# Layer 1's attention: dividing the head outputs by their sums behind the value product, instead of the probabilities before it

## The reference

```
q = (layernorm(x) @ wq + bq)  -> (16, 16 heads, 256, 8)
k = (ctx @ wk + bk)           -> (16, 16 heads, 64, 8)
v = (ctx @ wv + bv)           -> (16, 16 heads, 64, 8)
scores = q k^T / sqrt(8)
attn = softmax(scores, axis=-1)          # over 64 keys
out = attn v                             # (16, 256, 16 heads x 8 = 128)
x = x + tanh(g_xattn[1]) * (out @ wo + bo)
```

## Time and profile before

| | |
|---|---|
| median of 3 runs | 1190.56 us (1184.3 to 1193.06) |
| profiled execution | 1190.58 us, span 1188.8 us |
| mean granted clock of TensorE | 0.93 of full |
| busy: PE, DVE, ACT, POOL | 1069.7, 896.4, 578.6, 699.2 us |
| of POOL: L783, all four layers, 128 times | 215.6 us |
| layer 1: first and last residual update (L1307) | 212.08 and 400.96 us from the span's start |

### The profile page before, as it was taken

The page is one execution under the profiler, slowest core; times in us unless marked ns, Lnnn a source line. Parts: engine busy times, 40 slices in busy tenths (PEclk is TensorE's granted clock), DMA queues, the critical chain, the costliest instruction groups (busy, mean ns, idle before and its releaser), DMA issues. The chain is left out here.

```text
span 1188.8 us, 22954 instructions
## 1 busy us (share of the span) xinstructions
PE 1069.7 (90%) x6913; PEld 764.1 (64%) x6914; DVE 896.4 (75%) x2320; ACT 578.6 (49%) x1268; POOL 699.2 (59%) x979
## 2 busy tenths in 40 slices
PE   7999886888888899999999997999999999999643
PEld 5666574555555678957777766779966666666413
DVE  3999866788898668677788887667667777777395
ACT  2555443555555334455455553235445555554564
POOL 2555553666578764378766778844237677775203
PEclk7999996799889799999999999999999999999755
DMA  7997020000000016500000000025300000000002
GB/s 199 379 398 288 1 82 1 1 2 1 2 19 23 30 57 161 161 16 22 21 22 18 26 19 28 30 68 140 94 8 21 21 19 19 19 8 1 1 0 71
DMA packets 71551, 74.10 MB, mean 62 GB/s; under 512 B 9866, under 2 KB 57492, under 8 KB 71316
## 3 DMA queue, kind: packets, MB, share of 16 engines
q1 hardware_dynamic: 65300, 60.13, 15.8%
q0 software_dynamic: 6144, 12.64, 3.6%
HBM read 26.97 MB, written 45.78 MB: 61 GB/s over the span
## 5 line engine op out<-in xcount | busy, mean ns | idle before, releaser
L783 POOL TENSOR_TENSOR arena<-arena,zinv 128x1024 f32<-128x1024 f32 (+1 forms) x128 | 215.6, 1685 | 106.8 <-DVE zinv L1383 106.0
L1298 DVE TENSOR_REDUCE nmax<-S 128x16 f32<-128x1024 f32 (+1 forms) x128 | 138.8, 1084 | 101.9 <-PE S L2020 98.8
L2020 PEld LDWEIGHTS OX<-arena,pT 128*128 128x128 f32 x1280 | 151.6, 193 | 45.5 <-issue 44.9
L2020 PE MATMUL OX<-arena,pT 128*128 128x128 f32 x1280 | 166.3, 282 | 5.8 <-ACT pT L1072 5.7
L2020 PE MATMUL S<-arena,xT 128*128 128x512 f32 (+1 forms) x320 | 161.1, 602 | 1.1 <-ACT arena L1042 0.8
L1072 ACT ACTIVATE pT<-PT 128x512 f32<-128x512 f32 x224 | 124.6, 596 | 64.8 <-PE PT L2235 64.2
L2235 PE MATMUL PT<-ident,arena 128*128 128x128 f32 x896 | 132.5, 292 | 19.4 <-POOL arena L783 18.7
L2235 PEld LDWEIGHTS PT<-ident,arena 128*128 128x128 f32 x896 | 105.3, 148 | 54.6 <-POOL arena L783 37.9
L1358 DVE TENSOR_REDUCE zsum<-arena 128x16 f32<-128x1024 f32 (+1 forms) x128 | 137.7, 1076 | 0.0
L1349 DVE TENSOR_TENSOR arena<-S,nmax 128x1024 f32<-128x1024 f32 (+1 forms) x128 | 136.0, 1063 | 0.0
L1001 ACT ACTIVATE arena<-arena 128x1024 f32<-128x1024 f32 (+1 forms) x128 | 120.7, 943 | 6.9 <-DVE arena L1349 6.9
(11 more groups left out here) (374 smaller groups left out, 2324.6 us busy)
## 6 DMA issues: line engine op xcount, KB each, us to landing
x_sorted<-q_in SPq DMA_DIRECT2D x37, 387.0 KB, 4.8
y_sorted<-q_in SPq DMA_DIRECT2D x37, 384.0 KB, 4.7
arena<-x_sorted SPq DMA_DIRECT2D x62, 129.0 KB, 2.3
y_sorted<-arena SPq DMA_DIRECT2D x62, 128.0 KB, 2.1
x<-in_x SPq DMA_DIRECT2D x4, 512.0 KB, 7.8
out<-x SPq DMA_DIRECT2D x8, 256.0 KB, 2.3
moe_flat<-y_sorted,pos POOLq DMA_INDIRECT x96, 2.6
moe_flat<-in_L_gate_up_T SPq DMA_DIRECT2D x1, 1280.0 KB, 6.8
```

Source lines behind the costliest of these rows:

```text
L783: pool.tensor_tensor(pr, pr, z, ALU.mult).then_inc(s.probs_done, 1)
L1298: dve.tensor_reduce(nmax[:, p, 0:H], S[p][:, 0:W].rearrange("p (h k) -> p h k", h=H), AX.X, ALU.max, negate=True).then_inc(s.max_done, 1)
L2020: return pe.matmul(out, lhsT, rhs, start=start, stop=stop)
```

## The change

In layer 1 alone:

- POOL no longer multiplies the probabilities (32 instructions of 128 x 1024). `turn` waits for ACT's exponentials (`exp_done`) instead of for POOL.
- DVE no longer sums over the keys (L1358) and takes no reciprocal of 16 sums (L1383).
- PE multiplies the transposed probabilities a second time, behind the value product, with a constant of zeros and ones (`v1_ones`, 128 x 64): 8 matmuls of 32 columns into `GV[:, 128:256]`. Each of the 128 rows there is the sum of the head to which that row of `GV[:, 0:128]` belongs, so each head's sum is written 8 times. `attn_done` comes behind this second product.
- DVE, first thing in the next step, takes the reciprocal of 128 x 128 from `GV` into `attnT` and multiplies `GV[:, 0:128]` by it; `output1` waits for that (`sums_applied`). ACT's copy to `attnT` goes.
- POOL writes the constant between layer 0 and layer 1: one memset of 128 x 64 and four of 64 x 8.

```diff
@@ DVE, step t of layer 1 @@
+                    if a.small and is_tile(t - 1):
+                        heads = attnT[:, (r + 3) % 2, :]
+                        dve.wait_ge(s.attn_done, t)
+                        done(dve, s.out_done, a.tile0 + t - 3)
+                        dve.reciprocal(heads, GV[:, P:2 * P]).then_inc(s.head_sums_inverted, 1)
+                        dve.wait_ge(s.head_sums_inverted, t)
+                        dve.tensor_tensor(heads, GV[:, 0:P], heads, ALU.mult).then_inc(s.sums_applied, 1)
                     if a.small:
                         score_max()
...
-                    if is_tile(n):
+                    if is_tile(n) and not a.small:
                         T, p, j = a.tile0 + n, (r + 1) % 2, (r + 1) % 4
                         dve.wait_ge(s.exp_done, T + 1)
                         dve.tensor_reduce(zsum[:, p, 0:H], probs[:, j, 0:W].rearrange("p (h k) -> p h k", h=H), AX.X,
...
@@ POOL @@
-                    if is_tile(n):
-                        done(pool, s.zinv_done, a.tile0 + n)
+                    if is_tile(n) and not a.small:
+                        done(pool, s.sums_applied, a.tile0 + n)
                         pr = probs[:, (r + 1) % 4, 0:a.H * KEYS].rearrange("p (h k) -> p h k", h=a.H)
...
             pool.memset(v1, 0.0).then_inc(s.v1_zeroed, 1)
+            pool.memset(v1_ones[:, :], 0.0).then_inc(s.v1_zeroed, 1)
+            pool.wait_ge(s.v1_zeroed, 2)
+            for e in range(2):
+                for half in range(2):
+                    pool.memset(v1_ones[64 * e:64 * e + 64, 48 * half + 8 * e:48 * half + 8 * e + 8], 1.0).then_inc(s.v1_zeroed, 1)
+                    pool.wait_ge(s.v1_zeroed, 3 + 2 * e + half)
@@ ACT @@
-                    if a.small and is_tile(t):
-                        done(act, s.attn_done, t)
-                        done(act, s.out_done, a.tile0 + t - 2)
-                        act.activation(attnT[:, r % 2, :], GV[:, 0:P], ACT.Copy).then_inc(s.attn_evac, 1)
@@ PE: output1, heads1, turn @@
-                        pe.wait_ge(s.attn_evac, t)
+                        pe.wait_ge(s.sums_applied, a.tile0 + t)
...
+                        for c in range(8):
+                            rows = slice(32 * (c % 4), 32 * (c % 4) + 32)
+                            at = 32 * (c // 4)
+                            ins = mm(GV[rows, P:2 * P], v1_ones[:, at:at + 32], pT[:, r % 2, P * c:P * c + P],
                                      start=c < 4, stop=c >= 4)
                         ins.then_inc(s.attn_done, 1)
...
-                        pe.wait_ge(s.probs_done, a.tile0 + t + 1)
+                        if a.small:
+                            pe.wait_ge(s.exp_done, a.tile0 + t + 1)
+                        else:
+                            pe.wait_ge(s.probs_done, a.soft0 + t + 1)
```

More of the change, by code:

```diff
@@ L60, in __init__ @@
         self.small = dh < KEYS
+        self.soft0 = TILES * (l - (l > 1))
         self.gfill0 = BATCHES * sum(b.halves for b in before if not b.small)
@@ L172, in __init__ @@
         self.attn_done = sem("attn_done")
-        self.attn_evac = sem("attn_evac")
+        self.head_sums_inverted = sem("head_sums_inverted")
         self.kT_done = sem("kT_done")
@@ L194, in __init__ @@
         self.sum_done = sem("sum_done")
-        self.zinv_done = sem("zinv_done")
+        self.sums_applied = sem("sums_applied")
         self.probs_done = sem("probs_done")
@@ L430, in flamingo_program @@
         nmax = sb("nmax", [P, 2, 16])
+        v1_ones = sb("v1_ones", [P, 64])
         zsum = sb("zsum", [P, 2, 16])
@@ L1051, in filled @@
                                 act.wait_ge(s.sides_made, 4)
-                                act.wait_ge(s.v1_zeroed, 1)
+                                act.wait_ge(s.v1_zeroed, 6)
                             for e in range(2):
@@ L1379, in step @@
                         routing(a.l, t, 3)
[L1380 to L1383, removed]
+                    if is_tile(t + 1) and not a.small:
+                        dve.wait_ge(s.sum_done, a.soft0 + t + 2)
+                        done(dve, s.probs_done, a.soft0 + t - 1)
+                        dve.reciprocal(zinv[:, p, 0:H], zsum[:, p, 0:H]).then_inc(s.sums_applied, 1)
                     if between:
@@ L2185, in heads1 @@
                             ins = mm(GV[rows, 0:P], v1[:, (r // 2) % 2, at:at + 32], pT[:, r % 2, P * c:P * c + P],
+                                     start=c < 4, stop=c >= 4)
+                        for c in range(8):
+                            rows = slice(32 * (c % 4), 32 * (c % 4) + 32)
+                            at = 32 * (c // 4)
+                            ins = mm(GV[rows, P:2 * P], v1_ones[:, at:at + 32], pT[:, r % 2, P * c:P * c + P],
                                      start=c < 4, stop=c >= 4)
```

## The result

| | before | changed |
|---|---|---|
| median | 1189.47 us (1184.3 to 1193.06, 4 runs) | 1176.13 us (1173.19 to 1177.82, 4 runs) |
| profiled execution, span | 1190.58, 1188.8 us | 1177.82, 1176.1 us |
| mean granted clock | 0.93 | 0.951 |
| busy: PE, DVE, ACT, POOL | 1069.7, 896.4, 578.6, 699.2 us | 1058.7, 902.1, 571.4, 638.8 us |

The ratio of changed to before is 0.9895, with a 95% interval of 0.9866 to 0.9924: faster, by 1.0%. The forecast was 1178.6.

The account below looks back on a forecast made before the run. Bound: DVE's own work plus the ring through POOL. Tile 2 to 28: 43.2 + 99.0 + 2.6 = 144.8 against 158.9, -14.1; end +2.1; together -12.0 from 1190.58 gives 1178.6 us, range 1170 to 1190.

Parts of the forecast that it names:

- the ring through POOL: Layer 1: DVE's reciprocal, POOL's 1.90 us, PE's transposes, products and next scores, DVE's maxima close late, lengthening one step per pair.
- The bound: Layer 1's attention: before the change, DVE's own work plus the loop through POOL; afterwards DVE, with PE close behind.
- The wide reciprocal: DVE's added 128 x 128 reciprocal from PSUM: 0.84 us; rivals 1.2 us (14%), 1.96 us (8%), 0.28 us (13%).
- Steps with picks: DVE's step in layer 1 where it also makes picks: 5.60 us becomes 5.50, a pair 11.0.
- Steps without picks: DVE's step up to step 12 of layer 1, lacking up to three 0.13 us instructions: some 5.1 us, a pair 10.2.
- cover for POOL's inverse deviation: DVE's removed sums gave POOL time for its 0.72 us inverse deviation; lost cover costed at nothing, 0.15 us if just missed.
- PE's 10.8 for the early pairs: Four pairs before the picks go by PE: 2 x 4.58 + 0.62 for values + 2 x 0.5 for sums.
- the 2.6 for imperfect handovers: Allowance over tile 2 to 28 for imperfect handovers and two rank products on PE: 0.2 us a pair.
- The handover: PE's sums to DVE's division to PE's output product: DVE's 1.38 us is covered by PE's 1.65 us of other work.
- The clock: PE stays at the higher level throughout, about 1 us in 8 of 13 pairs; rival that it still falls: 1187, 13%.
- Opening: Start of layer 1's attention: 1.60 us wait ahead of first `turn` goes, two sums products at 0.88 us come: 0.
- Tail: Last three tiles of layer 1: exposed sums and division cost 3.5 us, a 1.40 us wait goes: +2.1.

Follow-up runs that it names:

- the test on the kernel before: Kernel before the change, with POOL multiplying only one of 16 heads by its inverse sum in layer 1: tile 2 to 28 took 141.84 us, ratio 0.9826.

## Why the prediction was right, and where not

The time was right (1176.13 for 1178.6, inside 1170 to 1190), and so was the mechanism in its main line: the ring through POOL went, the clock came up, DVE became the bound. That the time came so close is luck, since the terms that were off cancelled.

- **The bound, and the ring through POOL.** Right. Without POOL's multiplication the wait ahead of `turn` is gone, and the test on the kernel before puts some 17 us on that ring.
- **The wide reciprocal.** 0.945 us, for 0.84 from the slope of the narrow rows. The slope behind 16 columns is (945 - 245) / 112 = 6.25 ns a column, not 5.3. To the product's start it is 0.98, since the wait for its own result is 0.04 and not 0.1, and the product costs 0.20: 1.18 for the 1.19 of the sum.
- **Steps with picks.** Right: 5.28 to 5.60 over the last ten of the stretch, 5.48 on average, for 5.50.
- **Steps without picks.** This is the step that failed: "The sums also were cover for POOL's inverse deviation", which I "cost at nothing". They were cover, but for something else: POOL's key blocks and splits, which came behind its multiplication and so lay beside the maxima, the update and the statistics. Without both, they start with DVE's normalisations and hold them. Early steps took 5.67 to 5.86 instead of 5.1, all but one, and the six behind them, with picks too, 5.88 to 6.46. Holding them back gave 9.9 us, more than the whole 3.0 by which the stretch missed its forecast. So there was luck inside the stretch too: without the hold it is 137.8, 7.0 below the forecast, because PE's 10.8 for the early pairs (9.9 measured) and the 2.6 for imperfect handovers were both too much.
- **PE.** Sums product 0.55 for 0.5. A pair is 9.9, not 10.8, since the values only fill the time in which the value product waits for ACT's copies. PE is not "close behind".
- **The handover.** "Covered" was wrong, and by more than the 0.3 us that the prediction named as a sign of being wrong: PE waits for L1311 in 23 of the 26 steps, mostly 0.44 to 0.75 us. But these waits only show that DVE is slower; its reciprocal waits once in the stretch, for 0.15 us. That the ring is short rests on the division standing first.
- **The clock.** Right, 0.99. My reason, no idle stretches of 0.9 us left, holds only half: PE's waits of up to 0.89 us were still there.
- **Opening.** I gave it 0; it brought 2.6 us and what lies ahead of it 3.4, the latter about as much as the spread of that row. The first `turn` no longer waits, and the mean granted clock from 200 to 212 us is 0.84, where the kernel before had 0.55; from 212 to 225 it is 1.00 for 0.74. I had charged two sums products at the lower level there.
- **Tail.** +3.6 for +2.1: the exposed division was counted, the fall of the clock to 0.66 was not (worth at least 3.8 us, by the tail of the kernel with the sums run twice).

Against the forecast that is +3.0 in the stretch, +1.5 in the tail, +0.8 behind the layer and -6.0 in and ahead of the opening: the time came out so close because the last of these, which the sum had at 0, outweighed the others.

**Still open.** How much of the gain is the ring and how much the clock; what exactly in PE's work lets the clock stay up; and how much of the 3.4 us ahead of the opening the change made.

## What to carry to other kernels

An instruction taken off one engine may have been what kept two others apart: after such a change look for an instruction on the timeline that has become longer, not only for waits. A duration longer than the same instruction has elsewhere, with no wait in front of it, can be a hidden wait. And put a new handover first in the step of the engine that others wait for, unless at the end of a loop the waiting engine has other work that can go first.

## What the runs showed of the hardware

- A DVE `tensor_scalar` of 128 x 128 that reads SBUF (0.34 us) stood still for as long as a two-input product of POOL ran (1.17 us beside one of 1.04). The profile shows this as a longer instruction, with no idle time. A comparison of two SBUF tensors was held too (0.92 us for 0.22). A reciprocal, a product and a maximum that read PSUM were not touched by the same work, nor were statistics of an SBUF tile beside POOL's multiplication (0.28 us).
- A reciprocal of 128 x 128 in float32 out of PSUM takes 0.945 us, 3.3 times a product of that shape (0.29).
- Work on TensorE can cost nothing: with a product of 0.55 us a step added to the kernel before, the stretch was 5.4 us shorter and the granted clock 0.98 instead of 0.91. That it is shorter rests on one profile of each; that it is not longer by the product's own 14 us (26 x 0.55) is clear.
